# ScalarE's function table loads ahead of their unit's waits, with new engine orders and a new bank assignment, in a hybrid Mamba, RWKV and FFN block

## The reference

```python
x = x + attn_a(layernorm(x))      # Mamba, 512 inner channels, 16 states
x = x + ffn(layernorm(x))         # silu(x Wg) * (x Wu), then Wd; hidden 768
x = x + attn_b(layernorm(x))      # RWKV, 1024 channels
x = x + ffn(layernorm(x))

# attn_a: xs, z = split(x W_in); xc = silu(causal_conv4(xs) + b)
#   dt, B, C = split(xc W_x); dt = softplus(dt W_dt + b_dt)
#   h[t] = exp(dt[t] * A) * h[t-1] + dt[t] * B[t] * xc[t]      per channel and state
#   y = (sum over states of h*C + D*xc) * silu(z);  out = y W_out
# attn_b: R, K, V from three mixes of x[t-1] and x[t+1]
#   e = exp(clip(-w*(T-1-t) + K)); eu = exp(clip(U + K))
#   WKV = (cumsum(e*V) before t + eu*V) / (cumsum(e) before t + eu)
#   out = (sigmoid(R) * WKV) W_o + b_o
```

## Time and profile before

| | |
|---|---|
| median of 3 runs | 1805.29 us (1803.18 to 1805.94) |
| the profiled execution | 1803.37 us, span 1801.3 us |
| VectorE busy | 1523.5 us, 85% |
| TensorE busy | 1484.8 us, 82%; mean granted clock 0.918 |
| ScalarE busy | 1273.7 us, 71%, of it 304.1 us in 237 table loads |
| GpSimd busy | 1274.4 us, 71% |

### The profile page before, as it was taken

The page is one execution under the profiler, slowest core; times in us unless marked ns, Lnnn a source line. Parts: engine busy times, 40 slices in busy tenths (PEclk is TensorE's granted clock), DMA queues, the critical chain, the costliest instruction groups (busy, mean ns, idle before and its releaser), DMA issues. The chain is left out here.

```text
span 1801.3 us, 19199 instructions
## 1 busy us (share of the span) xinstructions
PE 1484.8 (82%) x4800; PEld 724.1 (40%) x4800; DVE 1523.5 (85%) x2045; ACT 1273.7 (71%) x2039; POOL 1274.4 (71%) x970
## 2 busy tenths in 40 slices
PE   4254487769889988989798888989897987999987
PEld 1011233234434453435444353444442552545364
DVE  3298889999989999998999998999999999984651
ACT  3567588776787768886788777877688576764742
POOL 0597987888588876888578886888588796650430
PEclk9676698989989999989999998999899998999999
DMA  7633445334345234533435234633345342211210
GB/s 225 224 117 130 148 134 184 97 129 132 130 122 191 70 129 156 170 115 123 140 122 175 91 116 140 206 100 124 123 135 159 102 137 83 94 44 51 62 41 29
DMA packets 163519, 225.21 MB, mean 125 GB/s; under 512 B 13457, under 2 KB 104082, under 8 KB 163410
## 3 DMA queue, kind: packets, MB, share of 16 engines
q1 hardware_dynamic: 163410, 223.99, 38.5%
HBM read 179.90 MB, written 39.85 MB: 122 GB/s over the span
## 5 line engine op out<-in xcount | busy, mean ns | idle before, releaser
L908 POOL TENSOR_TENSOR bu<-rep,bc 128x512 f32<-128x512 f32 x512 | 649.0, 1295 | 111.9 <-PE ps_y L1400 109.9
L1224 DVE TENSOR_TENSOR_SCAN ps_d<-ps_d,bu 128x512 f32<-128x512 f32 x384 | 458.2, 1214 | 62.6 <-POOL bu L908 51.7
L1068 ACT ACTIVATE ps_d<-rep,scale_a 128x512 f32<-128x512 f32 x512 | 337.6, 682 | 150.0 <-DVE bu L1231 130.3
L951 ACT ACT_TABLE_LOAD x237 | 304.1, 1283 | 108.0 <-PE ps_r L1349 34.1
L1349 PE MATMUL ps_r<-xT,wgu 128*128 128x512 f32 x768 | 360.0, 614 | 20.7 <-ACT hf L1090 6.9
L1349 PE MATMUL ps_r<-mix,wkv 128*128 128x512 f32 x512 | 251.3, 630 | 39.4 <-ACT yr L1115 12.7
L1231 DVE TENSOR_TENSOR bu<-ps_d,bc 128x512 f32<-128x512 f32 x384 | 253.3, 676 | 1.1
L1400 PE MATMUL ps_y<-bu,sel 128*32 128x512 f32 x1024 | 152.7, 671 | 106.1 <-DVE bu L1231 82.7
L1349 PEld LDWEIGHTS ps_r<-xT,wgu 128*128 128x128 f32 x768 | 144.9, 195 | 229.5 <-issue 222.3
L913 POOL TENSOR_TENSOR bu<-bu,bc 128x512 f32<-128x512 f32 x128 | 166.9, 1305 | 73.4 <-DVE bu L1224 72.6
L925 POOL TENSOR_TENSOR kv<-sums,kv 128x1024 f32<-128x1024 f32 x64 | 150.5, 2352 | 84.6 <-DVE sums L1310 66.8
(11 more groups left out here) (100 smaller groups left out, 2063.5 us busy)
## 6 DMA issues: line engine op xcount, KB each, us to landing
rep<-dd_scratch SPq DMA_DIRECT2D x128, 512.0 KB, 4.6
wgu<-gu_scratch SPq DMA_DIRECT2D x96, 256.0 KB, 2.7
bc<-bc_scratch SPq DMA_DIRECT2D x64, 256.0 KB, 3.2
dd_scratch<-dd SPq DMA_DIRECT2D x32, 512.0 KB, 2.9
wr<-w_r_dram SPq DMA_DIRECT2D x64, 128.0 KB, 2.3
win<-w_in_dram SPq DMA_DIRECT2D x64, 128.0 KB, 2.5
wo<-w_o_dram SPq DMA_DIRECT2D x16, 512.0 KB, 4.0
wkv<-w_k_dram SPq DMA_DIRECT2D x64, 128.0 KB, 2.3
```

The lines of the kernel that those rows point to most:

```text
L908: pool.tensor_tensor(bu[:, i % BU, :], rep[:, g % REP, 1, :], bc[:, 0, q, :], ALU.mult)\
L951: act.preload_act_table_set(name)
L1068: act.activation(ps_d[D_BANK[i]][:, :], rep[:, g % REP, 0, :], ACT.Exp, scale=scale_a[:, a, NQ * j + q:NQ * j + q + 1]).then_inc(decay_rea ...
L1224: dve.tensor_tensor_scan(states, d[:, :], bu[:, i % BU, :], 0.0, ALU.mult, ALU.add)\
```

## The change

In every unit of ScalarE that needs a set of tables, `need` moves from behind the waits to the head of the unit, and the semaphore increment in it is dropped. In `a_dt` it moves ahead of the two ACTIVATEs that work with either set, in `a_ln` ahead of one. All five orders are new (the sets of units are the same; of 872 units of TensorE 768 stand at another place, of 1224 of ScalarE 1110, none by more than 76 places), and so is the table of banks. With the new order ScalarE's set changes 201 times instead of 237. Three buffer tables (`D_BANK`, the number of buffers, the split between VectorE and GpSimd) are as before.

```diff
-        "hp_turn*2 p_in*4 p_xproj p_dt*4 p_in*4 p_y*2 hp_turn*2 p_in*3 p_y*2 p_in p_y p_in*2 p_y p_in p_y p_in p_y "
+        "hp_turn*2 p_in*5 p_xproj p_in*2 p_dt p_in p_dt*3 hp_turn*2 p_y*2 p_in*4 p_y*6 p_in*4 p_y p_xproj p_y "
...
                 if table[0] != name:
-                    act.sem_inc(carried.sem, 1)
                     act.preload_act_table_set(name)
                     table[0] = name
 
             def deviation(f, seq, i):
+                need("natural_log_exp_and_others")
                 part = slice(2 * (i % 2), 2 * (i % 2) + 2)
                 act.wait_ge(n_moments[f].sem, at(n_moments[f], seq, 2 * (i + 1)))
-                need("natural_log_exp_and_others")
...
                     elif unit == "a_dt":
 
+                        need("natural_log_exp_and_others")
                         src, bias = full(m_full, m, "p_dt", i), col("b_dt", i)
...
                         act.wait_ge(sp_abs.sem, at(sp_abs, m, i + 1))
-                        need("natural_log_exp_and_others")
                         act.activation(dtx, dtx, ACT.Exp, scale=-1.0).then_inc(sp_exp.sem, 1)
...
                     elif unit == "a_decay":
+                        need("natural_log_exp_and_others")
                         j, q, a = tile_of(i)
...
-                        need("natural_log_exp_and_others")
                         act.activation(ps_d[D_BANK[i]][:, :], rep[:, g % REP, 0, :], ACT.Exp,
...
                     elif unit == "fa_gate":
+                        need("silu_and_others")
                         stage, held = ffn_before("f", f)
                         src = full(f_full, f, "fp_gate", i)
                         if i == 0 and stage is not None:
                             act.wait_ge(down_read[stage].sem, at(down_read[stage], held, 2))
-                        need("silu_and_others")
...
                     elif unit == "a_rec":
+                        need("natural_log_exp_and_others")
                         act.wait_ge(dn_ready.sem, at(dn_ready, r, i + 1))
                         rec = take(act, unit, i, t)
-                        need("natural_log_exp_and_others")
```

More of the change, by code:

```diff
@@ new lines @@
+        "rp_down2 rp_down p_y rp_down2 p_k p_v p_y p_recept*2 p_k p_v p_recept p_k p_v p_recept p_y p_recept*2 p_k "
+        "p_v p_recept p_k p_v p_dt p_y p_k p_post*2 p_v p_wo fp_turn p_wo2 fp_turn2 p_y fp_turn fp_turn2 fp_gate "
+        "fp_up fp_gate fp_up p_y p_wo p_wo2 fp_gate fp_up fp_gate fp_up p_y fp_gate fp_up fp_gate fp_up p_y p_k "
+        "fp_down p_v p_dt p_y fp_down2 fp_down fp_down2 hp_turn*2 fp_turn p_wo p_wo2 fp_turn2 p_y fp_turn fp_turn2 "
+        "p_wo p_wo2 p_in rp_turn p_in p_k p_y rp_turn2 rp_turn rp_turn2 p_in*3 p_v p_in*2 p_y p_in p_xproj "
@@ new lines @@
+        "fp_turn p_wo2 p_y p_wo fp_turn2 fp_turn fp_turn2 p_wo2 p_in rp_turn p_in p_y p_in rp_turn2 rp_turn "
+        "rp_turn2 p_in*2 p_y p_in*2 p_xproj p_in p_dt p_y p_k p_v p_y p_recept p_k p_v p_recept*2 rp_gate rp_up "
+        "p_k p_v p_y rp_gate rp_up p_recept rp_gate rp_up p_y p_k p_v p_recept rp_gate p_y rp_up p_dt rp_gate "
+        "rp_up rp_gate p_y rp_up p_recept rp_down rp_down2 p_y rp_down rp_down2 p_post p_y p_post p_y p_recept p_k "
+        "p_v p_y p_recept p_k p_v fp_turn fp_turn2 fp_turn fp_turn2 p_wo p_wo2 fp_gate p_y fp_up fp_gate fp_up "
@@ new lines @@
+        "fp_gate fp_up p_k p_v fp_gate fp_up p_y p_wo p_wo2 fp_gate fp_up fp_gate p_y fp_up p_k fp_down p_v "
+        "fp_down2 fp_down p_y fp_down2 p_dt fp_turn p_dt hp_turn p_wo p_wo2 p_y fp_turn2 fp_turn fp_turn2 p_wo "
+        "p_wo2 hp_turn rp_turn p_in*2 p_k rp_turn2 rp_turn rp_turn2 p_in*2 p_v p_in*2 p_xproj p_y p_in*2 p_dt p_y "
+        "p_dt p_recept p_y p_k p_v p_recept p_y p_dt p_recept rp_gate rp_up p_k p_v rp_gate rp_up p_y p_recept "
+        "rp_gate rp_up p_k p_v p_recept rp_gate p_y rp_up rp_gate rp_up rp_gate rp_up p_y p_recept*2 rp_down "
@@ new lines @@
+        "rp_down2 rp_down rp_down2 p_y p_k p_v p_post*2 p_y p_recept p_k p_v p_dt p_wo p_wo2 fp_turn fp_turn2 "
+        "fp_turn fp_turn2 p_k p_y p_v fp_gate fp_up fp_gate fp_up fp_gate p_y fp_up fp_gate fp_up fp_gate fp_up "
+        "p_y fp_gate fp_up p_wo fp_down p_y p_wo2 p_k p_v fp_down2 p_y fp_down fp_down2 hp_turn*2 p_in*2 p_y "
+        "fp_turn p_in fp_turn2 fp_turn fp_turn2 p_in*2 p_wo p_wo2 p_in*2 p_wo p_wo2 p_xproj rp_turn p_y p_in p_k "
+        "p_v rp_turn2 rp_turn rp_turn2 p_dt p_recept p_y p_dt p_k p_v p_y p_recept*2 rp_gate rp_up p_k p_y p_v "
```

502 lines of the change are left out of this document (248 added, 254 removed), and 118 rows, old and new, of tables (BANKS, ORDER).

## The result

The changed kernel takes **1751.36 us** (median of 4 runs, 1748.87 to 1751.79) against 1805.62 for the kernel before (4 runs beside it, 1803.18 to 1806.99). The ratio is 0.970, with an interval of 0.968 to 0.972.

A forecast was written before the change was run, and what follows sets the result against it. VectorE was taken to bound the middle, TensorE the tail, a chain through ScalarE and GpSimd the head. Middle -15, head -5.5, statistics -2, tail -4 make -26.5 from 1803.37, 1776.9; median 1.9 higher: 1779 us, range 1758 to 1808.

The forecast's parts named there:

- The head: Up to the first scan: reordered p_in lets GpSimd's softplus chain start earlier, -5.5 us, bounds -8 and +2.
- the prediction's first objection: In the head, p_xproj now stands behind p_in 4, costing it 1.5 to 4 us if the weights land late.
- The statistics: hv_stats and hv_aggr of the second sequence move from between scans into VectorE's idle time in the head, -2 us.
- VectorE's waits on ScalarE in the middle: First scan to last p_y: waits for reciprocals and decays, 33.6 us, shrink with early loads, -15 us.
- VectorE's waits on TensorE: In the middle: spread thinly over TensorE's results, a reordering may move them either way; no gain counted.
- larger gain: Rival: ScalarE's lateness also delays TensorE by holding banks; 1760, or 1755 us with part of those waits; chance 0.18.
- The tail: After the last p_y, limited by TensorE: less idle time, one more p_k, -4 us, bounds -9 and +4.
- The feared crowding of K channels: Tail: K channels 3 to 7 of the last sequence come together, 30 us of VectorE work; p_wo may wait again.
- The price of a load: Each switch counted at 1.283 us of ScalarE work without a drain; 36 fewer make 46.2 us, not span.
- The slower one: Rival: in the middle, products meet their reciprocals too early when GpSimd is late; 1815 us at 1.7 each; chance 0.14.
- No change: Rival: the middle term is zero and the head collides; 1802 to 1808 us; chance 0.08.
- smaller gain: Rival: the loads were hidden already, so only head and tail gain; 1794 us; chance 0.12.

The follow-up runs named there:

- e2: Kernel before, old orders and banks, with its 237 table loads moved ahead of the waits: 1776.6 us, ratio 0.984.
- e1: Changed kernel's new orders and banks, with loads back behind the waits and the semaphore increment kept: 1787.6 us, ratio 0.989.
- e3: Old order with no table load but the first, Silu replaced by Relu and Tanh by Identity: 1755.2 us, ratio 0.972.
- e4: New order with no table load but the first, Silu replaced by Relu and Tanh by Identity: 1743.6 us, ratio 0.964.
- e9: e2 with only VectorE's v_skip, with its v_gate, moved at least five places behind the last v_hc it needs: 1786.6 us, ratio 0.989.
- e12: e2 with the first 36 a_recept computed with Identity in place of Tanh, leaving 201 loads: 1776.0 us, ratio 0.983.
- e14: e4 plus 36 loads, one in front of every eighth decay that follows a decay: 1749.8 us, ratio 0.970.
- e13: e4 plus 36 loads in front of a_rec and a_e units that follow a decay: 1759.7 us, ratio 0.975.
- e11: Changed kernel plus 36 redundant loads, one in front of every eighth decay that follows a decay: 1775.8 us, ratio 0.982.
- e5: Changed kernel plus 36 redundant loads in front of a_rec and a_e units that follow a decay: 1790.3 us, ratio 0.990.

## Why the prediction was right and where it was wrong

**The head: right.** Forecast -5.5, measured -5.3. TensorE's rows, the first `p_in` of the new place, then `p_xproj`, and further `p_in` and `p_dt` between and behind:

```profile
34.92 3.78 PE L1345 MATMUL ps_r<-xnT,win 128*128 128x512 f32 x4 [4.80 <-DMA win<-w_in_dram]
38.50 3.94 PE L1345 MATMUL ps_r<-xc,wx 128*96 128x512 f32 x8
42.27 3.60 PE L1345 MATMUL ps_r<-xnT,win 128*128 128x512 f32 x8
...
46.85 1.99 PE L1345 MATMUL ps_r<-xnT,win 128*128 128x512 f32 x4
```

`win` did land late, which pushed `p_xproj` from 35.44 to 38.50 as the prediction's first objection said; but it then took 3.94 us in place of 5.56, so TensorE ended `p_in` 7 at 48.84, near the 50 worked out, and GpSimd started its softplus chain at 51.92 (52 to 53 worked out). The first scan at 73.89 lies in the 73 to 75 that was named.

**The statistics: right.** Forecast -2, measured -2.4 of VectorE's busy time in the middle, 1.7 of it found again in the head.

**VectorE's waits on ScalarE in the middle: right in kind, and in size by luck.** Forecast -15, measured -15.0 over the three rows used (33.6 to 18.6), and early loads alone do it (18.4 in e2, but 32.9 in e1). The terms do not agree as the sum does. For the reciprocals 11 was forecast and 11.5 came (15.3 to 3.8), but of their 19 waits only 8, with 6.3 us, stood directly behind a load, so the gain is not 14 times the mean wait, as it was worked out. For the decays 9 was forecast and 3.5 came (18.3 to 14.8), although 13 of their 20 waits, with 11.1 us, did begin with a load. The 5 taken off for TensorE's results being late next made up for it, and in the changed kernel those results were late for less, not for more. What is missing is that the earlier trace rows were not all: with the smaller rows of the list the waits on ScalarE were 43.8, and they fell by 20.5. That is a gain of 5.5 that the sum had left out with rows too small to look at.

**VectorE's waits on TensorE: the step that failed.** The prediction wrote that they are "spread thinly over results of TensorE" and "a reordering may move it either way", and put zero. They fell by 23.6 us. That is nearly all of the 24.8 us by which the sum of -26.5 fell short of the 51.3 us between the two spans; the rest is the 5.5 above and 4 in the tail, against 7.8 of new waits for x. The early loads are not the cause by themselves (e2: 47.0), and the order is for 15 us of it (e1: 32.0). In all traces these waits come to 39 to 50 us in the five kernels with the old order and 23 to 32 in the eleven with the new one, whatever their loads (38.7 and 28 without any, e3 and e4). The changed kernel is the lowest of the eleven, so how much of its last 9 us is owed to early loads isn't settled. A higher clock isn't behind the 15: in e1's middle the granted clock is 0.92 as before, and TensorE is busy 1246.7 us for 1249.6. The rival named "larger gain" had this term, with a chance of 0.18 and 1755 as its time, but for the reason that ScalarE frees the banks sooner, and e2 refutes that reason as the main one. Which pairs of units in the new order take the 15 us off was not isolated: the order was only tried whole, except for e9, whose single move lost. So the cause of this term is shown down to the order as a whole and no further.

**The tail: right in sign, forecast at half its size.** Forecast -4, measured -8.0: 5.8 us less idle time (26.8 to 21.1), as many as the 5.8 taken, and 2.2 us less busy time (206.8 to 204.5, granted clock 0.96 and 0.98), where the prediction had added 1.8. TensorE's waits there on gates, reciprocals and exponentials are gone from the top of the list:

```profile
PE ps_r L1354 <- issue: 5.3, 2, 4.1
PE ps_r L1339 <- ACT kv L968: 3.8, 2, 3.0
```

The earlier trace rows had 2.1 and 2.0 us for them. But the idle time went elsewhere in part: the 4.1 us before `p_wo`, of which 1.3 was to go, are still there although no load stands in that chain any more, and the 6.8 us of the norms, which were to stay, are 3.8. The prediction tied the gain to 14 loads fewer. The trace has 27 and 15 loads in the tail, so 12 fewer, and e2 shows that it isn't their number: with all 27, early, its tail is 10.0 us shorter. The feared crowding of K channels can't be seen: e12, with the same order and loads as e2 in the tail, has 225.3 us there, as much as the changed kernel's 225.6.

**The price of a load: a step that held no single value.** "36 x 1.283 = 46.2 us less ScalarE work" is true of ScalarE and says nothing of the span: 36 loads were worth 0.6 us in the old order (e12), 6 and 16 (e14, e13) or 24 and 39 us (e11, e5) in the new one. The statement "with ScalarE mostly ahead" was too strong: it is ahead on the mean and late at many single places.

**Rivals.** The slower one is refuted: VectorE's waits of L1317 for its reciprocal are 3.8 us in the middle, and GpSimd's add still waited 64.4 us for VectorE's sums. "No change" and "smaller gain" are refuted by e2. Of the table load's price the Trainium skill ("ScalarE: Activation LUTs", What ACT_TABLE_LOAD costs) says that a drain of about 1380 ns belongs to each switch; after the change too, the ACTIVATE behind a switch starts 1.30 us after the load did (415.54 against 414.24 above), so the rows do not show it.

## What to carry to other kernels

Put a function table load ahead of its unit's waits wherever the engine order is fixed: here that alone gave 29 to 36 us of some 1800, and most per load for units that lie between two instructions of the limiting engine. Do not price a load, or its removal, at its duration or at zero: read at the place itself whether the engine stood idle before it and who waits behind it, since 36 loads were worth from 0.6 to 39 us by their place and by how full the engine was. And when a new order is forecast, add up all the small waits of the limiting engine by the engine waited for (here 44 and 47 us, with no single row above 16) and give each sum a bound of its own: here the new order took half of one of them.
